# Graph network kernel, one core: four early output panels in place of three, ring of six entries, finished panels 26 units apart

## The chip, the cores and the metric

The kernel runs on one core of one Trainium2 chip. The metric is the device time of one execution in microseconds, lower is better. The time given for a kernel is the median of several executions; the profile is of one further execution.

## What is computed

Node features x are 8192 x 128, the adjacency matrix adj is dense 8192 x 8192, all in float32 (256 MB for adj). Two layers follow each other, each with a residual and a layer norm. Cut to what matters:

```python
# layer 0
A = a * adj; A[i, i] += 1 - a              # a = alpha[0]
deg = A.sum(axis=1)
x1 = layernorm(x + relu((A @ x) / deg @ W.T + b))
# layer 1
t = logmap0(x1)                            # row norms, log
par = adj   * sigmoid(left_par[:, None] + right_par[None, :])
chi = adj.T * sigmoid(left_chi[:, None] + right_chi[None, :])
u = chi @ t + par @ t
out = layernorm(x1 + proj(expmap0(u)))     # row norms, tanh
```

Layer 0 reads adj once. Layer 1 needs each block of adj twice, once as it lies and once transposed, and it needs t, which is made from layer 0's output.

## The kernel before, in words

The output is cut into 8 panels of 1024 nodes (NPAN = 8, BP = 1024) and the other axis of adj into 64 tiles of 128 rows (UPP = 64).

**Layer 0** goes panel by panel through 256 pairs (two tiles of adj, 1 MB, PPP = 32 pairs a panel). Of a pair, TensorE makes 8 matmuls into Y (line 1024) and VectorE adds its 128x2048 elements to the degree sums dsum (line 777). After a panel's 32 pairs its sum is taken to yb (line 782), and a chain of small steps, the passage, makes degrees, residual, norm, logarithm, tangent and scores of the panel. The passage of panel r - 1 runs among the pairs of panel r: constants T_... give the pair q (0 to 31) before which each engine makes its step. In it xT, the next panel's feature block, is loaded at T_LOADX and scaled at T_SCALEX (line 522), and the row of scores that a panel needs is written to HBM at tick 19 and read back to all partitions (two transfers of 512 KB) at tick 21 for each early panel.

**Layer 1** is cut into 512 units: a unit is one 128 x 1024 tile of the sum of both attention products for an output panel p. ScalarE makes two sigmoids (lines 613 and 627), GpSimd multiplies one by adj as it lies (line 477), VectorE multiplies the other by the transposed tile (line 868) and adds the two (line 879), and TensorE multiplies the sum with t into outp (4 matmuls, line 1092). Two units share two loads of 1 MB, "nat" and "trn".

**Early units.** A unit can start as soon as the t of its tile's panel is there. So EARLY = 3 output panels take units while layer 0 still runs: plan() places at most one unit at a pair, in groups of 8 to 24 units of one panel; at each group's end VectorE adds outp to acc (line 890, evacuate), and TensorE starts the next group only after that. With three early panels, 8, 12, 24, 32, 32, 24 and 24 units lie at the pairs of panels 1 to 7: 156 in all (N_EARLY). The other 356 run after layer 0, the first 12 of them as two more early groups, the rest as whole panels 3 to 7 with the last tiles of the early panels between them. The passage of panel 7 runs among the first 40 or so of these units, at twice the number of units.

**After layer 0.** Each finished output panel goes through a final chain (row norms, tanh, residual, layer norm, store), whose steps are given as F_... units after its base. FINALS holds the bases: 232, 266, 304, 338, 376, 410, 448 and 512.

**Loads.** SyncE issues all loads of adj in the order of use, each into the next entry of a ring of RING = 7 entries of 1 MB, and waits before each until the load that held this entry has been used: a pair by both line 1024 and line 777, a nat by both its units' products on GpSimd, a trn by those on VectorE. After layer 0, three more entries (EXTRA, where x lay) join.

Of the kernel before, what the change touches and what calls it, by code (L numbers as in the profile page):

```python
# [11 lines left out]
P = 128  # L12
D = 128
BP = 1024
NPAN = N // BP
TPP = BP // P
# [13 lines left out]
UPP = N // P  # L30
PPP = UPP // 2
PAIRS = NPAN * PPP
EARLY = 3
RING = 7
EXTRA = 3
CB = 3
KB = 3
# [6 lines left out]
(T_EVAC, T_FOLD, T_DEG, T_INV, T_LIN, T_RES, T_STATS, T_STD, T_RSTD, T_X1, T_SQ, T_NRM, T_LOGA, T_LN, T_FAC, T_XT,  # L44
 T_TURN, T_XTT, T_PRP, T_PRCR, T_ROWS, T_COPY, T_LOADL) = (0, 0, 1, 2, 3, 4, 5, 6, 7, 8, 9, 10, 11, 12, 13, 14,
                                                           16, 16, 17, 18, 18, 19, 21)
T_LOADX, T_SCALEX = 6, 10
T_UNITS = 20
T_OWN = 23

# [1 line left out]
def early_groups():  # L52

    groups = []
    for a in range(NPAN - 1):
        for p in range(min(EARLY, a + 1)):
            groups.append((p, range(0 if p == a else a * TPP, (a + 1) * TPP), a))
    return groups

def plan():

    unit_at, units, ends, waiting = {}, [], [], []
    groups = early_groups()
    for k, (p, tiles, a) in enumerate(groups):
        for jt in tiles:
            waiting.append((k, p, jt, (a + 1) * PPP + (T_OWN if p == a else T_UNITS)))
    for g in range(PAIRS):
        if waiting and waiting[0][3] <= g:
            k, p, jt, _ = waiting.pop(0)  # L70
            unit_at[g] = len(units)
            units.append((k, p, jt))
    n_early = len(units)
    units += [(k, p, jt) for k, p, jt, _ in waiting]
    order = []
    for k in range(EARLY, NPAN):
        order.append((k, range(UPP)))
        if k - EARLY < EARLY:
            order.append((k - EARLY, range((NPAN - 1) * TPP, UPP)))
    for p, tiles in order:  # L80
        groups.append((p, tiles, NPAN - 1))
        units += [(len(groups) - 1, p, jt) for jt in tiles]
    for n, (k, _, _) in enumerate(units):
        if n + 1 == len(units) or units[n + 1][0] != k:
            ends.append(n)
    return unit_at, units, n_early, groups, ends
# [17 lines left out]
def finals():  # L104
    out, base = [], {}
    for k, (p, tiles, a) in enumerate(GROUPS):
        if a == NPAN - 1:
            base[p] = ENDS[k] + 1
    for p in range(EARLY, NPAN):
        out.append((p, base[p]))  # L110
        if p - EARLY < EARLY:
            out.append((p - EARLY, base[p] + 34))
    return out

FINALS = finals()
FIN_OF = {p: k for k, (p, _) in enumerate(FINALS)}
F_EVAC, F_TURN, F_SLOT, F_COPY, F_SQUARE, F_ROOT, F_FLOOR, F_INV, F_RSTD, F_TANH, F_CHAIN, F_NORM, F_SCALE, F_ADD, \
    F_STATS, F_AGGR = 3, 2, 4, 5, 6, 15, 17, 18, 18, 19, 21, 20, 29, 31, 33, 42
F_LOADX = 16  # L120
F_STORE = 42
L_ROOT, L_RSTD, L_NORM = 47, 49, 52
F_STEPS = 8
# [63 lines left out]

def row_plan():
    out, use, end_of = {}, [0, 0, 0], [None, None, None]  # L190
    buf = 0
    for k, (p, tiles, a) in enumerate(GROUPS):
        if a < NPAN - 1:
            b = p
            if (p, "early") not in out:
                use[b] += 1
                out[(p, "early")] = (b, use[b], None)
        else:
            b = buf % 3
            buf += 1  # L200
            use[b] += 1
            out[k] = (b, use[b], end_of[b])
        end_of[b] = ENDS[k]
    return out
# [53 lines left out]
def adj_resnorm_kernel(nc, x_g, xT, g_blk, a_blk, WT, b_row, alpha, w_par, b_par, w_chi, b_chi, out):  # L258
    with ExitStack() as ctx:
        def sb(name, shape):  # L260
            return ctx.enter_context(nc.sbuf_tensor(name, shape, F32))

        def sem(name):
            return ctx.enter_context(nc.semaphore(name))
# [2 lines left out]
        xA = sb("xA", [P, N])  # L267
        xtA = sb("xtA", [P, N])
        acc = sb("acc", [P, EARLY * BP])
        scores = sb("scores", [P, 3, 2, BP])  # L270
        chi_few = sb("chi", [P, CB, BP])
        keys_few = sb("keys", [P, KB, BP])
        dsum = sb("dsum", [P, 2 * BP])
        yb = sb("yb", [P, BP])
        res = sb("res", [P, BP])
        xTt = sb("xTt", [P, BP])
        rows = xTt[0:2, :]

        prcr = sb("prcr", [P, UPP * 2])
# [58 lines left out]
        bpc2_ready = sem("bpc2_ready")  # L338
        x_in = [sem(f"x_in{G}") for G in range(NG)]
        r_in = [sem(f"r_in{e}") for e in range(RING + EXTRA)]  # L340
        l_in = [sem(f"l_in{k}") for k in range(3)]
        l0_used = sem("l0_used")
        deg_added = sem("deg_added")
        folded = sem("folded")
# [6 lines left out]
        h_ready = sem("h_ready")  # L351
# [14 lines left out]
        prp_ready = sem("prp_ready")  # L366
# [34 lines left out]
        def _(sp):  # L401
# [15 lines left out]
            def load_x1(k):  # L417
                p, _ = FINALS[k]
                if k < 2:
                    sp.wait_ge(x1_out, 16 * NPAN)  # L420
                    sp.wait_ge(xt_ready, NPAN)
                    sp.wait_ge(h_ready, NPAN)
                else:
                    sp.wait_ge(out_done, 16 * (k - 1))
                sp.dma_start(x1f[k % 2][:, :], x1_d[p]).then_inc(x1f_in[k % 2], 16)
# [86 lines left out]
        def _(act):  # L512

            def load_xT(r):
                if r > 0:
                    act.wait_ge(h_ready, r)
                act.dma_start(yb[:, :], xT[:, r * BP:(r + 1) * BP]).then_inc(xT_in, 16)

            def scale_xT(r):
# [16 lines left out]

            def squares(r):

                act.wait_ge(rows_out, 16 * r)
                for k in range(TPP):  # L540
                    ins = act.activation(xTt[:, k * D:(k + 1) * D], res[:, k * D:(k + 1) * D], ACT.Square,
                                         accum_out=ss[:, k:k + 1])
                ins.then_inc(ss_ready, 1)
# [614 lines left out]
```

## Time and profile before

| what | value |
|---|---|
| median of 3 runs | 2269.03 us (2265.76 to 2272.19) |
| profiled execution, device time | 2268.08 us |
| its span in the profile | 2266.1 us |
| PE busy | 1958.9 us, 86% of the span |
| VectorE (DVE) busy | 1992.6 us, 88% |
| ScalarE (ACT) busy | 1333.1 us, 59% |
| GpSimd (POOL) busy | 1307.4 us, 58% |
| moved by the DMA engines | 839.16 MB, 370 GB/s over the span |

The shares are averages over a first part (layer 0, up to 1269 us) and a second part whose limits differ, so that none of them names what binds; the stages have to be read one by one. The busy time of PE is modelled: matmuls overlap, and a busy PE is not PE at its peak.

### The profile page before, as it was taken

The page shows a single profiled execution, that of the slowest core. Times are in us where ns is not written, and L with a number is a line of the kernel's source. Part 1 is how long each engine was busy: PE and PEld are TensorE (multiplying, and loading weights), DVE is VectorE, ACT ScalarE, POOL GpSimd, SP SyncE. Part 2 cuts the span into 40 slices and gives each one's busy share as a digit, 9 for nine tenths or more (in the row PEclk, how much of TensorE's full clock was granted, in tenths as well). Part 3 has the DMA queues.
Part 4 walks back from the last instruction along what each step waited for, and adds up shares of the span by engine and source line. Part 5 has one row for each costly group of instructions (what it writes and reads, how often), then busy time and mean ns, then how long its engine had stood idle before and what let it go on. Part 6 is the DMA issues. An engine that isn't in the chain of part 4 may idle for free.

```text
span 2266.1 us, 17503 instructions
## 1 busy us (share of the span) xinstructions
PE 1958.9 (86%) x4652; PEld 827.4 (37%) x4652; DVE 1992.6 (88%) x1899; ACT 1333.1 (59%) x1622; POOL 1307.4 (58%) x544
## 2 busy tenths in 40 slices
PE   8999999999989989999999867887777777777774
PEld 3444444444434434444444322232232222222221
DVE  6676879989988988899899987999999999999995
ACT  0022134534543363354354587998889889898986
POOL 0001215325444444433433767989898998999995
PEclk9999999999999999999999999999999999999998
DMA  9988989999989898899999998999999999999994
GB/s 377 369 295 319 349 309 410 352 357 392 365 342 397 338 349 341 350 363 359 362 362 358 409 405 311 409 409 409 409 408 409 405 409 401 403 409 402 409 403 180
DMA packets 227568, 839.16 MB, mean 370 GB/s; under 512 B 14464, under 2 KB 22912, under 8 KB 227472
## 3 DMA queue, kind: packets, MB, share of 16 engines
q1 hardware_dynamic: 220672, 817.94, 92.7%
q10 hardware_dynamic: 6800, 20.13, 2.4%
q8 instruction: 38, 0.62, 0.1%
q14 instruction: 58, 0.48, 0.1%
HBM read 829.56 MB, written 8.45 MB: 370 GB/s over the span
## 4 chain that ended last, share of the span: by engine, by line
PE 34%; POOL 17%; issue 16%; DVE 15%; ACT 13%; DMA 4%; DVEq 0%; ACTq 0%; POOLq 0%; SPq 0%
PE ps L1024 25%; POOL chi L477 13%; PE ps L1092 7%; DVE dsum L777 6%; ACT chi L613 4%; DVE ps L868 4%; POOL xA L477 3%; ACT ps L627 3%; DMA ring<-in_a_cols 2%; DVE keys L879 1%; DMA ring<-in_g_blk 1%; ACT L613 1%; ACT xA L613 1%; DMA xA<-in_a_cols 1%; ACT dsum L657 1%
## 5 line engine op out<-in xcount | busy, mean ns | idle before, releaser
L477 POOL TENSOR_TENSOR chi<-chi,ring 128x1024 f32<-128x1024 f32 x322 | 812.3, 2536 | 741.0 <-ACT chi L613 620.9
L1092 PE MATMUL ps<-keys,xtA 128*128 128x512 f32 x1720 | 848.3, 620 | 198.7 <-DVE keys L879 169.4
L1024 PE MATMUL ps<-ring,xA 128*128 128x512 f32 x2048 | 921.7, 600 | 20.3 <-DMA ring<-in_g_blk 15.2
L627 ACT ACTIVATE ps<-scores,prcr 128x1024 f32<-128x1024 f32 x512 | 568.0, 1109 | 506.3 <-DVE keys L879 487.3
L777 DVE TENSOR_TENSOR dsum<-dsum,ring 128x2048 f32<-128x2048 f32 x240 | 595.8, 2482 | 23.8 <-DMA ring<-in_g_blk 18.4
L868 DVE TENSOR_TENSOR ps<-ps,ring 128x1024 f32<-128x1024 f32 x442 | 540.4, 1223 | 67.0 <-ACT ps L627 54.1
L879 DVE TENSOR_TENSOR keys<-ps,chi 128x1024 f32<-128x1024 f32 x430 | 526.5, 1224 | 59.2 <-issue 28.4
L1024 PEld LDWEIGHTS ps<-ring,xA 128*128 128x128 f32 x2048 | 390.2, 193 | 511.7 <-issue 489.7
L1092 PEld LDWEIGHTS ps<-keys,xtA 128*128 128x128 f32 x1720 | 315.3, 195 | 699.3 <-issue 659.8
L613 ACT ACTIVATE chi<-scores,prcr 128x1024 f32<-128x1024 f32 x430 | 488.2, 1135 | 7.5 <-DMA scores<-plcl_d 3.5
L477 POOL TENSOR_TENSOR chi<-chi,xA 128x1024 f32<-128x1024 f32 x108 | 254.5, 2374 | 36.5 <-ACT chi L613 33.6
L1092 PE MATMUL ps<-xA,xtA 128*128 128x512 f32 x328 | 159.7, 609 | 46.2 <-DVE xA L879 46.2
L477 POOL TENSOR_TENSOR xA<-xA,ring 128x1024 f32<-128x1024 f32 x50 | 118.8, 2375 | 11.5 <-ACT xA L613 9.0
L1092 PEld LDWEIGHTS ps<-xA,xtA 128*128 128x128 f32 x328 | 56.4, 190 | 146.7 <-issue 146.7
L879 DVE TENSOR_TENSOR xA<-ps,xA 128x1024 f32<-128x1024 f32 x82 | 100.4, 1225 | 3.7 <-POOL xA L477 1.0
L470 POOL TENSOR_TENSOR dsum<-dsum 128x1024 f32<-128x1024 f32 x8 | 18.8, 2351 | 136.9 <-DVE dsum L777 109.0
L613 ACT ACTIVATE xA<-scores,prcr 128x1024 f32<-128x1024 f32 x82 | 93.0, 1135 | 0.4 <-ACT xTt L567 0.4
L526 ACT ACT_TABLE_LOAD x8 | 10.3, 1283 | 140.2 <-PE ps L1040 140.1
L868 DVE TENSOR_TENSOR ps<-ps,xA 128x1024 f32<-128x1024 f32 x70 | 85.5, 1222 | 4.5 <-ACT ps L627 2.6
L477 POOL TENSOR_TENSOR xA<-xA 128x1024 f32<-128x1024 f32 x32 | 76.0, 2374 | 7.0 <-ACT xA L613 5.0
L773 DVE TENSOR_TENSOR dsum<-ring 128x1024 f32<-128x1024 f32 x16 | 25.2, 1618 | 29.4 <-PE ps L1033 18.3
L557 ACT ACTIVATE xtA<-res,small 128x128 f32<-128x128 f32 x64 | 19.6, 388 | 48.5 <-DVE small L839 48.5
(98 smaller groups left out, 618.2 us busy)
## 6 DMA issues: line engine op xcount, KB each, us to landing
ring<-in_g_blk SPq DMA_DIRECT2D x477, 1024.0 KB, 9.9
ring<-in_a_cols SPq DMA_DIRECT2D x186, 1024.0 KB, 12.3
xA<-in_a_cols SPq DMA_DIRECT2D x70, 1024.0 KB, 18.0
xA<-in_g_blk SPq DMA_DIRECT2D x35, 1024.0 KB, 18.2
scores<-plcl_d ACTq DMA_DIRECT2D x22, 512.0 KB, 6.8
xA<-in_x_g SPq DMA_DIRECT2D x16, 256.0 KB, 10.4
yb<-in_xT ACTq DMA_DIRECT2D x8, 512.0 KB, 6.7
x_d<-res ACTq DMA_DIRECT2D x8, 512.0 KB, 7.5
```

What stands on the lines that cost most here:

```text
L470: pool.tensor_tensor(out=dsum[:, 0:BP], in0=dsum[:, 0:BP], in1=dsum[:, BP:2 * BP], op=ALU.add).then_inc(folded, 1)
L477: pool.tensor_tensor(out=chi(n), in0=chi(n), in1=half(t, n), op=ALU.mult).then_inc(m2_ready, 1)
L557: ins = act.activation(xtA[:, at:at + D], res[:, k * D:(k + 1) * D], ACT.Copy, scale=fac[:, k:k + 1])
L613: act.activation(chi(n), scores[:, row, 1, :], ACT.Sigmoid, bias=prcr[:, 2 * jt + 1:2 * jt + 2]).then_inc(c_ready, 1)
L627: act.activation(slots[s], scores[:, row, 0, :], ACT.Sigmoid, bias=prcr[:, 2 * jt:2 * jt + 1]).then_inc(p_ready, 1)
L657: ins = act.activation(uT[:, i * D:(i + 1) * D], uN[:, i * D:(i + 1) * D], ACT.Square, accum_out=s_ss[:, k * TPP + i:k * TPP + i + 1])
L773: dve.tensor_tensor(out=half(dsum, h), in0=half(t0, h), in1=half(t, h), op=ALU.add) \
L777: dve.tensor_tensor(out=dsum[:, :], in0=dsum[:, :], in1=t, op=ALU.add).then_inc(deg_added, 1)
L868: dve.tensor_tensor(out=s, in0=s, in1=half(t, n), op=ALU.mult).then_inc(m1_ready, 1)
L879: dve.tensor_tensor(out=keys(n), in0=slots[SLOT_OF_UNIT[n][0]], in1=chi(n), op=ALU.add).then_inc(k_ready, 1)
L1024: ins = pe.matmul(Y[:, h * BANK:(h + 1) * BANK], xA[:, tile * D:(tile + 1) * D], t[:, tt * BP + h * BANK:tt * BP + (h + 1) * BANK], start= ...
L1092: ins = pe.matmul(outp[:, h * BANK:(h + 1) * BANK], xtA[:, jt * D:(jt + 1) * D], keys(n)[:, h * BANK:(h + 1) * BANK], start=begins, stop=i ...
```

## The change

A fourth output panel takes units among layer 0's pairs: 8, 12, 24, 32, 32, 32 and 32 units at the pairs of panels 1 to 7, 172 in all. 340 units run after layer 0, the first 52 of them in early groups (seven group ends against two before). LATE_BEHIND puts the early panels' last tiles behind panels 4 and 5, two behind each, and the bases of the final chains become 288, 314, 340, 368, 394, 420, 448 and 512.

The room for acc (4 KB more a partition) and for a fourth buffer of score rows (8 KB) comes from the ring, which goes from 7 to 6 entries (8 KB), and from xTt, which now shares yb's room (4 KB). Since xTt and yb are one, xT is loaded at tick 22 in place of 6 and scaled at 27 in place of 10, and some waits are added. The steps of the final chains move: the scaling on GpSimd from 29 to 27, the residual from 31 to 29, the statistics from 33 to 31, the load of x1 from 16 to 24.

```diff
--- before.py
+++ after.py
@@ -30,8 +30,8 @@
 UPP = N // P
 PPP = UPP // 2
 PAIRS = NPAN * PPP
-EARLY = 3
-RING = 7
+EARLY = 4
+RING = 6
 EXTRA = 3
 CB = 3
 KB = 3
@@ -44,7 +44,7 @@
 (T_EVAC, T_FOLD, T_DEG, T_INV, T_LIN, T_RES, T_STATS, T_STD, T_RSTD, T_X1, T_SQ, T_NRM, T_LOGA, T_LN, T_FAC, T_XT,
  T_TURN, T_XTT, T_PRP, T_PRCR, T_ROWS, T_COPY, T_LOADL) = (0, 0, 1, 2, 3, 4, 5, 6, 7, 8, 9, 10, 11, 12, 13, 14,
                                                            16, 16, 17, 18, 18, 19, 21)
-T_LOADX, T_SCALEX = 6, 10
+T_LOADX, T_SCALEX = 22, 27
 T_UNITS = 20
 T_OWN = 23
 
@@ -56,6 +56,11 @@
         for p in range(min(EARLY, a + 1)):
             groups.append((p, range(0 if p == a else a * TPP, (a + 1) * TPP), a))
     return groups
+
+
+
+LATE_BEHIND = {EARLY: (0, 1), EARLY + 1: (2, 3)}
+F_APART = 26
 
 
 def plan():
@@ -75,8 +80,8 @@
     order = []
     for k in range(EARLY, NPAN):
         order.append((k, range(UPP)))
-        if k - EARLY < EARLY:
-            order.append((k - EARLY, range((NPAN - 1) * TPP, UPP)))
+        for p in LATE_BEHIND.get(k, ()):
+            order.append((p, range((NPAN - 1) * TPP, UPP)))
     for p, tiles in order:
         groups.append((p, tiles, NPAN - 1))
         units += [(len(groups) - 1, p, jt) for jt in tiles]
@@ -108,16 +113,16 @@
             base[p] = ENDS[k] + 1
     for p in range(EARLY, NPAN):
         out.append((p, base[p]))
-        if p - EARLY < EARLY:
-            out.append((p - EARLY, base[p] + 34))
+        for i, early in enumerate(LATE_BEHIND.get(p, ())):
+            out.append((early, base[p] + (i + 1) * F_APART))
     return out
 
 
 FINALS = finals()
 FIN_OF = {p: k for k, (p, _) in enumerate(FINALS)}
 F_EVAC, F_TURN, F_SLOT, F_COPY, F_SQUARE, F_ROOT, F_FLOOR, F_INV, F_RSTD, F_TANH, F_CHAIN, F_NORM, F_SCALE, F_ADD, \
-    F_STATS, F_AGGR = 3, 2, 4, 5, 6, 15, 17, 18, 18, 19, 21, 20, 29, 31, 33, 42
-F_LOADX = 16
+    F_STATS, F_AGGR = 3, 2, 4, 5, 6, 15, 17, 18, 18, 19, 21, 20, 27, 29, 31, 39
+F_LOADX = 24
 F_STORE = 42
 L_ROOT, L_RSTD, L_NORM = 47, 49, 52
 F_STEPS = 8
@@ -187,7 +192,7 @@
 
 
 def row_plan():
-    out, use, end_of = {}, [0, 0, 0], [None, None, None]
+    out, use, end_of = {}, [0] * EARLY, [None] * EARLY
     buf = 0
     for k, (p, tiles, a) in enumerate(GROUPS):
         if a < NPAN - 1:
@@ -196,7 +201,7 @@
                 use[b] += 1
                 out[(p, "early")] = (b, use[b], None)
         else:
-            b = buf % 3
+            b = buf % EARLY
             buf += 1
             use[b] += 1
             out[k] = (b, use[b], end_of[b])
@@ -267,13 +272,14 @@
         xA = sb("xA", [P, N])
         xtA = sb("xtA", [P, N])
         acc = sb("acc", [P, EARLY * BP])
-        scores = sb("scores", [P, 3, 2, BP])
+        scores = sb("scores", [P, EARLY, 2, BP])
         chi_few = sb("chi", [P, CB, BP])
         keys_few = sb("keys", [P, KB, BP])
         dsum = sb("dsum", [P, 2 * BP])
         yb = sb("yb", [P, BP])
         res = sb("res", [P, BP])
-        xTt = sb("xTt", [P, BP])
+
+        xTt = yb
         rows = xTt[0:2, :]
 
         prcr = sb("prcr", [P, UPP * 2])
@@ -338,7 +344,7 @@
         bpc2_ready = sem("bpc2_ready")
         x_in = [sem(f"x_in{G}") for G in range(NG)]
         r_in = [sem(f"r_in{e}") for e in range(RING + EXTRA)]
-        l_in = [sem(f"l_in{k}") for k in range(3)]
+        l_in = [sem(f"l_in{k}") for k in range(EARLY)]
         l0_used = sem("l0_used")
         deg_added = sem("deg_added")
         folded = sem("folded")
@@ -420,6 +426,8 @@
                     sp.wait_ge(x1_out, 16 * NPAN)
                     sp.wait_ge(xt_ready, NPAN)
                     sp.wait_ge(h_ready, NPAN)
+                    sp.wait_ge(prp_ready, NPAN)
+                    sp.wait_ge(rows_out, 16 * NPAN)
                 else:
                     sp.wait_ge(out_done, 16 * (k - 1))
                 sp.dma_start(x1f[k % 2][:, :], x1_d[p]).then_inc(x1f_in[k % 2], 16)
@@ -514,6 +522,9 @@
             def load_xT(r):
                 if r > 0:
                     act.wait_ge(h_ready, r)
+                    act.wait_ge(prp_ready, r)
+                    act.wait_ge(rowp_ready, r)
+                    act.wait_ge(rows_out, 16 * r)
                 act.dma_start(yb[:, :], xT[:, r * BP:(r + 1) * BP]).then_inc(xT_in, 16)
 
             def scale_xT(r):
@@ -536,7 +547,7 @@
 
             def squares(r):
 
-                act.wait_ge(rows_out, 16 * r)
+                act.wait_ge(h_ready, r + 1)
                 for k in range(TPP):
                     ins = act.activation(xTt[:, k * D:(k + 1) * D], res[:, k * D:(k + 1) * D], ACT.Square,
                                          accum_out=ss[:, k:k + 1])
```

## Rows read from the trace of the kernel before

**Rows 1.** The page, part 1: busy time and share of each engine.
```profile
PE 1958.9 (86%) x4652; PEld 827.4 (37%) x4652; DVE 1992.6 (88%) x1899; ACT 1333.1 (59%) x1622; POOL 1307.4 (58%) x544
```

**Rows 2.** Windows, panels 3 to 7: length, busy (instructions) by engine, PEclk, DMA share, GB/s.
```profile
core 0: us, PE busy (x) PEld busy (x) DVE busy (x) ACT busy (x) POOL busy (x), PEclk, DMA share, GB/s
...
388.00:551.90 163.90, 161.46 (x413) 73.58 (x412) 147.57 (x131) 71.79 (x92) 67.89 (x26) 0.99 0.96 371
551.90:741.10 189.20, 178.50 (x445) 80.16 (x444) 167.89 (x147) 89.00 (x108) 87.71 (x34) 0.97 0.94 367
741.10:936.60 195.50, 183.26 (x447) 81.96 (x445) 171.19 (x150) 88.96 (x108) 87.75 (x34) 0.96 0.91 351
936.60:1102.90 166.30, 162.07 (x413) 74.52 (x412) 152.08 (x132) 71.78 (x92) 65.69 (x26) 0.99 0.92 357
1102.90:1269.20 166.30, 161.88 (x412) 74.06 (x413) 152.39 (x132) 71.79 (x92) 68.23 (x26) 0.99 0.93 359
```

**Rows 3.** Windows after layer 0: end of the last passage, and the steady part.
```profile
1350.00:1370.00 20.00, 15.36 (x28) 5.86 (x26) 19.34 (x23) 16.57 (x22) 14.83 (x7) 0.83 0.90 329
1370.00:1390.00 20.00, 12.81 (x35) 5.75 (x34) 13.44 (x12) 13.11 (x14) 13.25 (x7) 0.83 0.73 275
1390.00:1410.00 20.00, 16.17 (x44) 6.33 (x44) 15.42 (x15) 14.90 (x15) 14.96 (x7) 1.00 0.87 339
...
1430.00:1460.00 30.00, 24.68 (x52) 8.51 (x50) 29.55 (x26) 28.28 (x27) 30.00 (x14) 1.00 1.02 409
...
1493.00:2073.70 580.70, 439.63 (x926) 161.71 (x925) 546.64 (x577) 516.10 (x609) 529.92 (x228) 0.97 1.02 406
```

**Rows 4.** DMA issues from 1500 to 2200 us: count, size, median us to landing.
```profile
ring<-in_g_blk SPq DMA_DIRECT2D x104, 1024.0 KB, 18.5
```

**Rows 5.** DVE's timeline: the last panel's sum, and the last unit's key.
```profile
1269.21 1.27 DVE L782 SCALAR_TENSOR_TENSOR yb<-ps,alph,yb 128x1024 f32<-128x1024 f32 x1
...
2238.28 1.23 DVE L879 TENSOR_TENSOR keys<-ps,chi 128x1024 f32<-128x1024 f32 x1
```

**Rows 6.** Windows: pairs q = 14 to 21 of panels 5 and 6; pairs 20 to 30 of panel 7.
```profile
826.70:884.90 58.20, 50.58 (x125) 22.17 (x124) 46.38 (x38) 25.72 (x30) 26.79 (x11) 0.91 0.85 323
1019.10:1051.50 32.40, 32.03 (x93) 14.85 (x92) 29.09 (x25) 12.02 (x17) 7.69 (x3) 1.00 0.87 320
...
1211.00:1264.30 53.30, 53.30 (x125) 23.34 (x124) 51.35 (x31) 21.89 (x20) 28.84 (x11) 1.00 1.00 396
```

**Rows 7.** Waits of PE in panel 5's pairs 14 to 21: total, times, longest.
```profile
PE ps L1092 <- DVE acc L890: 4.5, 1, 4.5
PE ps L1060 <- DVE prcr L843: 3.1, 1, 3.1
```

**Rows 8.** Lines, panel 5 by form: busy, mean ns, then idle before.
```profile
L477 POOL TENSOR_TENSOR chi<-chi,ring 128x1024 f32<-128x1024 f32 x32 | 85.4, 2677 | 100.9 <-ACT chi L613 94.5 <-DMA ring<-in_a_cols 6.4
L777 DVE TENSOR_TENSOR dsum<-dsum,ring 128x2048 f32<-128x2048 f32 x30 | 76.0, 2533 | 0.0
```

**Rows 9.** One line's instructions, whole span: min/median/max ns.
```profile
L777 DVE TENSOR_TENSOR dsum<-dsum,ring x240: 2255/2292/4309, 18.0 to 1265.9; 128x2048 f32<-128x2048 f32 x120
...
L477 POOL TENSOR_TENSOR chi<-chi,xA x108: 2338/2366/2477, 1284.5 to 2219.2; 128x1024 f32<-128x1024 f32 x108
...
L890 DVE TENSOR_TENSOR acc<-ps,acc x15: 1211/1219/1225, 378.9 to 1312.9; 128x1024 f32<-128x1024 f32 x15
```

**Rows 10.** SyncE's timeline in panel 5: issues of the loads of pairs 11 and 12.
```profile
798.47 0.37 SPq L452 DMA_DIRECT2D ring<-in_g_blk  x1
806.90 0.37 SPq L452 DMA_DIRECT2D ring<-in_g_blk  x1
```

**Rows 11.** Issues at 798.47 and 806.90 us alone: us to landing.
```profile
ring<-in_g_blk SPq DMA_DIRECT2D x1, 1024.0 KB, 8.6
ring<-in_g_blk SPq DMA_DIRECT2D x1, 1024.0 KB, 4.8
```

**Rows 12.** Timeline of panel 5: PE at pair 11, GpSimd at pair 9's unit, xT's scaling.
```profile
803.20 3.67 POOL L477 TENSOR_TENSOR chi<-chi,ring 128x1024 f32<-128x1024 f32 x1 [2.05 <-ACT chi L613]
...
804.00 1.13 ACT L522 ACTIVATE yb<-yb,oma 128x1024 f32<-128x1024 f32 x1
...
807.42 3.60 PE L1024 MATMUL ps<-ring,xA 128*128 128x512 f32 x8
```

**Rows 13.** Waits of SyncE's queue in panel 5: total, times, longest.
```profile
SPq L452 <- DVE ps L868: 49.6, 14, 7.4
SPq L411 <- DVE dsum L777: 43.8, 14, 5.9
SPq L452 <- PE ps L1024: 32.4, 12, 8.5
SPq L452 <- POOL chi L477: 29.3, 8, 8.0
```

## The prediction

> **What bounds the kernel now.** I read the page first: VectorE 88% and TensorE 86% busy [rows 1], no engine full, so the stages have to be taken one by one. The timeline of VectorE cuts the run in two: layer 0 ends with the last panel's sum at 1269.2 us, the last unit's sum starts at 2238.3 us [rows 5], and the rest, up to 2266.1 us, is the last panel's final chain, which the change leaves alone.
>
> The windows after layer 0 show one limit. In the 580.7 us from 1493 on the DMA engines are saturated (share 1.02, 406 GB/s) while no engine is over 94% busy [rows 3]. A load waits 18.5 us from issue to landing [rows 4]. At the 409 GB/s of the window from 1430 to 1460 us [rows 3] a load of 1.0486 MB takes 2.563 us of the stream, so seven loads stand in the queue: the ring of ten is far deeper than this stage needs. A unit needs 1 MB there, and 2.563 us is its price. Only from 1350 to 1410 us, under the last passage, does the stream fall short (329, 275 and 339 GB/s [rows 3]): there the ring is full and the engines are what is late.
>
> Layer 0's windows are different. Panels 6 and 7 with 24 units take 166.3 us each, panels 4 and 5 with 32 units 189.2 and 195.5 us; the DMA share is 0.91 to 0.96, the TensorE clock 0.96 to 0.99 of full [rows 2]. In a stretch with no passage TensorE is busy all of 53.3 us with 125 matmuls, 0.426 us each [rows 6]: a pair with a unit (12 matmuls) costs 5.1 us, a pair alone 3.4. Two loads cost 5.13 us, so the two limits lie on top of each other there. In the passage's stretch neither holds: TensorE waits for engines.
>
> **The units that move: what they cost and what they save.** 16 units go from the late part to pairs, 8 to panel 6 and 8 to panel 7; panels 1 to 5 keep their counts.
>
> Saved after layer 0: 16 x 2.563 = 41.0 us, since that part is stream-bound behind the passage and the final chains move the same bytes as before.
>
> Added in layer 0: the 8 pairs that have no unit in panels 6 and 7 are q = 12 to 19, the densest part of the passage; with TensorE's two pairs of lag the products fall into q = 14 to 21. With units these 8 pairs took 58.2 us in panel 5, without 32.4 us in panel 6 [rows 6]: 25.8 us for 8 units, where 8 x 4 matmuls x 0.426 = 13.6 us would be TensorE's own work. The difference is waits: TensorE stands 4.5 us for a group's evacuation and 3.1 us behind the score step, once each [rows 7], and the clock is 0.91 there against 1.00. The whole panels carry the same message, and since the change makes panels 6 and 7 into copies of panels 4 and 5, I take those: the new panel 6 has group ends at q = 22 and 30, none at 14, like panel 4 (ends at 6 and 30), so 189.2 - 166.3 = 22.9 us; the new panel 7 has ends at 6, 14, 22 and 30 like panel 5, so 195.5 - 166.3 = 29.2 us. Together +52.1 us. Moved units thus cost 3.3 us each in place of 2.56. Bounds: 2 x 13.6 = 27.3 us if the units only cost TensorE's work, 2 x 29.2 = 58.4 us if both panels are like panel 5.
>
> Part of this price shows as two engines that slow each other: in panel 5 GpSimd's product takes 2677 ns and VectorE's dsum add 2533 ns on the mean [rows 8], against medians of 2366 and 2292 ns [rows 9]. The Trainium skill (SBUF, State Buffer, section Who interferes with whom) says that a VectorE instruction with two SBUF inputs and a GpSimd instruction that reads SBUF exclude each other for a whole instruction; the dsum add is such an instruction, while the two VectorE steps of a unit have one input in PSUM. By that rule the late part is free of it and each moved unit buys one possible collision, of at most a GpSimd product; the trace agrees in direction with the means just named. It speaks against the move, and its price is already inside the 52.1 us.
>
> **The ring of six in layer 0.** A load goes out when the entry that it takes is free. With one entry less and the same users, load i takes the entry that load i + 1 takes now, so it goes out when load i + 1 goes out in this trace. Where the next issue follows within 2.6 us nothing is lost, as the stream would not have been quicker. Panel 5 has one place where it matters: the load of pair 11 is issued at 798.47 us, the next, that of pair 12, only at 806.90 us [rows 10], when GpSimd has finished its product for the unit of pair 9 (803.20 + 3.67 = 806.87 [rows 12]) and so freed a nat entry. The first lands after 8.6 us, at 807.07; TensorE starts pair 11 at 807.42 [rows 11, 12], with 0.35 us to spare. With six entries it goes out at 806.90 and with the 4.8 us that a load issued then takes [rows 11] lands at 811.7 us: TensorE and the dsum add behind it stand 4.3 us. Nothing gives this back, since TensorE has 5.1 us of work a pair afterwards and the later loads wait for users that are late too. SyncE waits for VectorE, TensorE and GpSimd in turn [rows 13], so every entry is held to the end of its use. The passage repeats in every panel, the normalisation and squares on ScalarE that make GpSimd late at that place too, so I count 4.3 us in each of panels 3 to 7: +21.5 us. Bounds: nothing, if the six entries suffice after all (panels 1 and 2, with few units, I count so); and 5 x (4.3 + 2.1) = 32 us, should each panel have a second place half as costly, some 40 with a clock that falls after the waits.
>
> After layer 0 the ring is 9 entries instead of 10. It is full when the passage ends, so the stream starts its last, saturated run one load behind: +2.6 us. Further on, with seven loads in flight now, six suffice: nothing. If that cover were gone, each final chain would cost a load, 8 x 2.6 = 20 us.
>
> **Group ends.** An evacuation is 1.219 us on VectorE [rows 9]. During the late passage there are now five more ends of early groups. VectorE is 19.3 of 20 us busy in one of the three windows and 13.4 and 15.4 in the next [rows 3], so some of the five fall into its idle time: I take 3 us. Bounds: 0, and 5 x (1.2 + 0.4) = 8.
>
> **Transfers.** The fourth early panel's score rows are one more MB, at tick 21 of panel 4, where stream and TensorE are even: up to 2.6 us. The load of xT (0.5 MB, 1.3 us) moves from tick 6, where the stream has room, to tick 22, where it has none, in four panels of 32 units: up to 5 us, less what the earlier stretch gains. I take +2, bounds 0 and 8. ScalarE's scaling at tick 27 (1.13 us [rows 12]) and the waits added to load_xT, load_x1 and squares are on work that is done ticks before: ScalarE is 89.0 of 195.5 us busy in panel 5 [rows 2]. Nothing; without that cover, one wait of some 3 us a panel.
>
> **Final chains 26 apart.** GpSimd needs 26 x 2.366 us [rows 9] plus two operations of that size for its chain, 66 us; the stream needs 26 x 2.563 + 2.56 us for x1 and the store, 69.2 us. The stream still sets the pace. VectorE: 546.6 us busy for 216 units and six chains [rows 3], 2.53 us a unit with chains in; 26 x 2.53 = 66 us, and a little more with chains denser: also below. Nothing; bound 10 us if steps of two chains meet in the queues.
>
> **The sum.** Against the profiled execution of 2268.08 us: + 52.1 - 41.0 + 21.5 + 2.6 + 3 + 2 = + 40.2, 2308.3 us. The median of the runs is 1 us higher, so 2309 us.
>
> **The rivals.**
> 1. *The ring of six costs nothing* and only the rest holds: 52.1 - 41.0 + 2.6 + 3 + 2 = +18.7, 2288 us. For it: the stalls rest on one place that I read with 4.3 us, and xT's scaling leaves ScalarE just ahead of it, which brings GpSimd's product forward by up to 1.1 us. Against: the product that frees the entry waits for sigmoids that the ring doesn't touch. Chance 0.2.
> 2. *Faster: the moved units cost TensorE's work alone*, 27.3 us, against 41.0 saved, because the waits of panels 4 and 5 in the passage belong to where their groups end and not to the units. With the other terms and a harmless ring, 27.3 - 41.0 + 2.6 + 2 = -9, about 2260 us. It decides below (41.0 - 8)/16 = 2.1 us a unit. Against: panel 4 has no group end at q = 14 and still is 22.9 us over panel 6. Chance 0.12; a mixture that lands within 0.3% 0.08.
> 3. *The late part loses its saturation*: chains that overlap at 26 units, nine entries. Another 10 to 20 us on the forecast, 2325 us. Against: seven loads in the queue. Chance 0.1.
>
> My forecast, both the panels' price and the ring's, has 0.5.
>
> **How the numbers follow.** The forecast's own range, from the bounds of its terms, is 2292 to 2328 us. For 8 in 10 it has to take in the first rival and reach toward the second: 2268 to 2330. Within 0.3% (6.8 us, about what a measurement of this kernel can tell from no change) I give 0.08, faster 0.12, slower 0.5 + 0.2 + 0.1 = 0.8.
>
> **What would show it.** In the profile after: panels 6 and 7 of 190 to 200 us (175 to 180 would be rival 2); panels 3, 4 and 5 4 us longer than 163.9, 189.2 and 195.5 with TensorE waiting for ring<-in_g_blk near q = 11 (unchanged: rival 1); layer 0's last sum at about 1345 us; from there to the end 962 us in place of 997, with the stream at 405 to 409 GB/s once the passage is over (less: rival 3). The prediction is wrong if the passage's waits don't grow with the units, or if ScalarE without xT's scaling at tick 10 frees the entries in time.

## The result and the profile after

The changed kernel takes 2298.07 us (median of 4 runs, 2293.92 to 2302.52) against 2270.61 us for the kernel before beside it: ratio 1.0116, 95% interval 1.0097 to 1.0135. It is slower, by 26 us by the ratio (27 by the two medians), on the side that was forecast and inside the range; the forecast was 40 us. The profiled execution's span is 2292.1 us against 2266.1, so the profiles differ by 26.0 us too and can be read against each other term by term.

The page of the changed kernel, part 1 (answers to [rows 1]):

```profile
PE 1963.1 (86%) x4656; PEld 825.3 (36%) x4656; DVE 1990.1 (87%) x1903; ACT 1334.7 (58%) x1622; POOL 1318.1 (58%) x544
```

No engine got much more work: the busy times differ by some 4 us at most on PE, VectorE and ScalarE, and by 11 on GpSimd, which is idle for 42% of the span. The 26 us are for the most part waits. Windows of panels 3 to 7 of the changed kernel, as in [rows 2]:

```profile
391.43:562.85 171.42, 162.51 (x414) 73.31 (x412) 148.77 (x132) 71.85 (x92) 68.45 (x26) 0.99 0.92 357
562.85:754.68 191.83, 178.58 (x445) 80.02 (x444) 168.41 (x147) 89.16 (x108) 89.47 (x34) 0.97 0.93 361
754.68:944.69 190.01, 177.65 (x443) 79.71 (x442) 171.26 (x149) 89.14 (x108) 89.77 (x34) 0.97 0.93 359
944.69:1132.48 187.79, 177.91 (x446) 80.06 (x445) 166.83 (x148) 89.15 (x108) 87.81 (x34) 0.97 0.94 365
1132.48:1323.83 191.35, 179.22 (x445) 80.07 (x444) 171.65 (x150) 89.03 (x108) 91.72 (x34) 0.97 0.92 358
```

Panel by panel against [rows 2]: +7.5, +2.6, -5.5, +21.5, +25.1 us, and 3 to 4 us in panels 0 to 2. VectorE's timeline gives the two cuts, the last panel's sum and the last unit's key (answers to [rows 5]):

```profile
1323.83 1.27 DVE L793 SCALAR_TENSOR_TENSOR yb<-ps,alph,yb 128x1024 f32<-128x1024 f32 x1
...
2264.32 1.23 DVE L890 TENSOR_TENSOR keys<-ps,chi 128x1024 f32<-128x1024 f32 x1
```

Layer 0 ends 54.6 us later (1323.8 - 1269.2), and from there to the last key it is 940.5 us in place of 969.1, 28.6 us less; the tail is the same 27.8 us. 54.6 - 28.6 = 26.0.

The late part, in windows of the changed kernel (the last passage, the time just after it, the steady part) as in [rows 3]:

```profile
1430.00:1460.00 30.00, 22.56 (x61) 9.73 (x60) 21.14 (x19) 16.31 (x16) 14.73 (x7) 0.89 0.74 281
1488.00:1518.00 30.00, 23.58 (x50) 8.23 (x49) 29.59 (x26) 27.57 (x27) 30.00 (x14) 1.00 1.03 409
1518.00:2100.00 582.00, 439.75 (x929) 159.54 (x929) 540.50 (x571) 517.41 (x610) 525.39 (x226) 0.98 1.02 407
```

The stream is as saturated as before once the passage is over (407 GB/s, share 1.02): nine entries and chains 26 units apart did not take that away. Under the passage it falls to 281 GB/s, as it fell to 275 in the kernel before [rows 3].

### The profile page after: what moved, and what is told of

It reads as the page before. It is cut to its first block, busy times and chain, and to the rows that moved or that the text cites. A ratio compares the mean times of both kernels' runs of the same rounds, so it can differ in the third digit from the quotient of the medians.

```text
span 2292.1 us, 17535 instructions
## 1 busy us (share of the span) xinstructions
PE 1963.1 (86%) x4656; PEld 825.3 (36%) x4656; DVE 1990.1 (87%) x1903; ACT 1334.7 (58%) x1622; POOL 1318.1 (58%) x544
## 4 chain that ended last, share of the span: by engine, by line
PE 27%; issue 18%; POOL 18%; DVE 17%; ACT 15%; DMA 5%; DVEq 0%; ACTq 0%; POOLq 0%; SPq 0%
PE ps L1035 20%; POOL chi L485 14%; DVE ps L879 6%; DVE dsum L788 6%; ACT chi L624 5%; PE ps L1103 5%; POOL xA L485 3%; ACT ps L638 3%; DMA ring<-in_a_cols 2%; DMA xA<-in_a_cols 2%; DVE keys L890 1%; DMA ring<-in_g_blk 1%; ACT L624 1%; ACT xA L624 1%; PE ps L1071 1%
## 5 line engine op out<-in xcount | busy, mean ns | idle before, releaser
L485 POOL TENSOR_TENSOR chi<-chi,ring 128x1024 f32<-128x1024 f32 x349 | 886.5, 2553 | 758.2 <-ACT chi L624 474.0
L1103 PE MATMUL ps<-keys,xtA 128*128 128x512 f32 x1736 | 852.9, 616 | 196.2 <-DVE keys L890 161.8
L879 DVE TENSOR_TENSOR ps<-ps,ring 128x1024 f32<-128x1024 f32 x398 | 486.7, 1223 | 81.0 <-ACT ps L638 43.2
L485 POOL TENSOR_TENSOR chi<-chi,xA 128x1024 f32<-128x1024 f32 x85 | 200.0, 2365 | 30.5 <-ACT chi L624 26.9
L1103 PE MATMUL ps<-xA,xtA 128*128 128x512 f32 x312 | 153.5, 615 | 44.6 <-DVE xA L890 44.6
L879 DVE TENSOR_TENSOR ps<-ps,xA 128x1024 f32<-128x1024 f32 x114 | 139.3, 1222 | 8.6 <-ACT ps L638 6.2
L890 DVE TENSOR_TENSOR xA<-ps,xA 128x1024 f32<-128x1024 f32 x78 | 95.5, 1225 | 3.3 <-POOL xA L485 0.8
L485 POOL TENSOR_TENSOR xA<-xA 128x1024 f32<-128x1024 f32 x27 | 63.9, 2368 | 3.4 <-DMA xA<-in_a_cols 2.8
L784 DVE TENSOR_TENSOR dsum<-ring 128x1024 f32<-128x1024 f32 x16 | 18.9, 1222 | 29.3 <-PE ps L1044 18.3
## 6 DMA issues: line engine op xcount, KB each, us to landing
xA<-in_a_cols SPq DMA_DIRECT2D x56, 1024.0 KB, 16.1
```

The lines of the kernel that those rows point to most:

```text
L485: pool.tensor_tensor(out=chi(n), in0=chi(n), in1=half(t, n), op=ALU.mult).then_inc(m2_ready, 1)
L784: dve.tensor_tensor(out=half(dsum, h), in0=half(t0, h), in1=half(t, h), op=ALU.add) \
L879: dve.tensor_tensor(out=s, in0=s, in1=half(t, n), op=ALU.mult).then_inc(m1_ready, 1)
L890: dve.tensor_tensor(out=keys(n), in0=slots[SLOT_OF_UNIT[n][0]], in1=chi(n), op=ALU.add).then_inc(k_ready, 1)
L1103: ins = pe.matmul(outp[:, h * BANK:(h + 1) * BANK], xtA[:, jt * D:(jt + 1) * D], keys(n)[:, h * BANK:(h + 1) * BANK], start=begins, stop=i ...
```

## The experiments

Each was timed beside the kernel before, whose median was 2271.2, 2272.7 and 2268.3 us in three groups of runs. Ratios carry their 95% interval. Times of single panels come from one profile of each kernel, and two profiles of the same kernel can differ: layer 0 ends at 1323.8 us in the first profile of the changed kernel and at 1332.6 in the second (after_again). A difference of a few us in one panel is read as one only where several profiles show it.

| run | what it is | ratio | interval |
|---|---|---|---|
| e1_ring6 | 3 early panels, 6 entries | 1.0079 | 1.0061 to 1.0096 |
| e2_late_xt | 3 early, 7 entries, late xT | 0.9984 | 0.9973 to 0.9996 |
| e3_ring6_late_xt | 3 early, 6 entries, late xT | 1.0087 | 1.0072 to 1.0102 |
| e4_four_ring7 | 4 early, 7 entries | 1.0073 | 1.0056 to 1.0090 |
| after_again | the changed kernel | 1.0109 | 1.0090 to 1.0128 |
| e5_withheld | changed, 16 units held back | 1.0116 | 1.0096 to 1.0136 |
| e6_merged | changed, 3 group ends fewer | 1.0081 | 1.0062 to 1.0099 |
| e7_three_withheld | before, 16 units held back | 0.9936 | 0.9920 to 0.9952 |
| e8_withheld_merged | the same, ends merged | 0.9948 | 0.9932 to 0.9965 |
| e9_hold_12_16 | before, pairs 12 to 16 free | 1.0084 | 1.0068 to 1.0100 |
| e10_hold_15_19 | before, pairs 15 to 19 free | 1.0101 | 1.0085 to 1.0118 |
| e11_held_merged_late_xt | e8 with late xT | 0.9941 | 0.9927 to 0.9956 |

**The parts of the change, one by one.** e1 changes one line of the kernel before, `RING = 7` to `RING = 6`.

> The kernel before with six ring entries and nothing else. My theory (each of panels 3 to 7 gets one TensorE stall of 4.3 us near pair 11, nothing gives it back, and the late stream starts one load behind): layer 0's end 21 us later, the whole +24 us, ratio 1.0105. Rival (panels 4 and 5 already stand for loads at pairs 12 and 13, 4 us each, and the new stall takes the place of that one): panels 4 and 5 unchanged, panels 3, 6 and 7 +4 to +7 us each, the whole +15 us, ratio 1.0065. Rival (six entries suffice): +3 us, ratio 1.001.

+18 us, between the theory's 24 and the rival's 15. Windows of its panels 3 to 7:

```profile
391.27:561.56 170.29, 162.46 (x414) 73.24 (x412) 148.73 (x131) 71.78 (x92) 68.84 (x26) 0.99 0.94 360
561.56:751.68 190.12, 179.38 (x445) 80.41 (x444) 170.97 (x147) 88.99 (x108) 89.69 (x34) 0.97 0.93 362
751.68:944.74 193.06, 179.70 (x442) 80.89 (x443) 172.34 (x150) 88.97 (x108) 89.92 (x34) 0.96 0.91 351
944.74:1115.63 170.89, 164.09 (x414) 74.28 (x413) 152.46 (x132) 71.78 (x92) 68.69 (x26) 0.98 0.90 347
1115.63:1288.23 172.60, 162.57 (x411) 73.64 (x410) 151.39 (x132) 71.77 (x92) 70.98 (x27) 0.98 0.92 356
```

The 24-unit panels 3, 6 and 7 pay 6.4, 4.6 and 6.3 us, the 32-unit panels 4 and 5 +0.9 and -2.4. The first three panels together take 3.3 us more, where nothing was counted. So the loss exists and has about its forecast size, but in a panel filled with units it is given back: the rival of the shifted stall, by its panels if not quite by its total. From layer 0's end on, the run is 3.5 us longer (2.6 were forecast).

e2 and e3 load xT late, with seven and with six entries:

```diff
-T_LOADX, T_SCALEX = 6, 10
+T_LOADX, T_SCALEX = 22, 27
...
-        xTt = sb("xTt", [P, BP])
+        xTt = yb
```

and the waits of the change's diff on load_xT, load_x1 and squares.

> The kernel before with xT loaded at tick 22 and scaled at tick 27, xTt in yb's room, seven entries. My theory (a hidden transfer is moved from one covered place to another): within 3 us of before. Rival (xT's 0.5 MB at tick 6 and its scaling at tick 10 are part of what makes the loads of pairs 12 and 13 late in panels 4 and 5): these two panels 4 us shorter each, the whole -8 us, ratio 0.9965.

> Both: six entries and the late xT, three early panels. If the two act apart, the sum of the two runs before it. My theory: +24 us, ratio 1.0105. Rival of a shifted stall: +7 to +15 us, ratio 1.003 to 1.0065, with TensorE waiting near pair 10 and no longer at 12 and 13.

The late xT is 3.6 us faster by the ratio with seven entries, and makes no measurable difference with six (1.0079 and 1.0087). The rival's place is right: pairs 12 and 13 together take 11.3 us in e2's panel 4 and 10.9 in its panel 5, in place of 14.5 and 14.2. But other waits of the same panels grow, TensorE's for a group's evacuation in panel 5 from 4.5 to 6.1 us, and the panels take 188.6 and 194.7 us, not 4 us less than 189.2 and 195.5. What makes the 3.6 us stays open.

e3 against e2 is also the ring's price with late xT and three early panels: 1.0087 - 0.9984, 23 us. By panels (3 to 7: +6.6, 0.0, -3.7, +7.4, +6.5 us, and +2.3 before them) it repeats what e1 shows.

e4 is the changed kernel with RING = 7. The room comes from score rows: three buffers, the early units of panel 3 reading panel 0's rows. The kernel leaves out the early read-back of panel 3's own rows, 1 MB in panel 4. In that panel the step from pair 22 to pair 23 takes 6.6 us in the changed kernel and 5.1 to 5.2 in the kernel before and in e4, so some 1.4 us of the difference between e4 and the changed kernel may be this transfer and not the ring.

```diff
-RING = 6
+RING = 7
...
-            b = p
+            b = p % 3
...
-                if tick == T_LOADL and r < EARLY:
+                if tick == T_LOADL and r < 3:
```

> The changed kernel with seven ring entries; the room comes from score rows, of which three buffers stay: the early units of panel 3 read panel 0's score rows, and panel 3's own are not read back early. My theory (ring 24 us, moved units and group ends the rest): 2274 us, +4 us against before, panels 6 and 7 still over 185 us. Rival (the ring costs less than 10 us, the moved units make most of the loss): +15 us or more, ratio 1.007 or more. A ratio below 1 would say that the moved units gain and the ring alone makes the change slower.

> The changed kernel once more, on the chip of the runs beside it, so that they can be compared with it. Ratio 1.0116 within its interval. Against the run with four early panels and seven entries (1.0073) it gives what the seventh entry is worth in the changed kernel: 10 us by the ratios, 4 us by the two profiles.

With seven entries four early panels still cost 17 us against before and 20 against e2, where the theory had 4: the ring alone doesn't explain the loss. The seventh entry is worth 8 us here (1.0109 - 1.0073; the intervals just touch) where it is worth 18 with three early panels (e1), 23 with late xT (e3 against e2): the two losses overlap. The profiles agree: e4's panels 3 to 7 take 165.2, 188.8, 191.1, 190.6 and 196.3 us. Six entries cost panel 3 6.3 us and panel 4 3.0, and make panels 5, 6 and 7 1.1, 2.8 and 5.0 us shorter; with after_again in place of the first profile it is 9.8 and 2.8 dearer, then 1.2, 2.3 and 2.5 shorter. Layer 0 ends 3 and 12 us behind e4's.

**The moved units.** e5 (in the changed kernel, panels 6 and 7) and e7 (in the kernel before, panels 4 to 7, of which 4 and 5 had such units) leave pairs 12 to 19 without units:

```diff
-        if waiting and waiting[0][3] <= g:
+        if waiting and waiting[0][3] <= g and not (g // PPP >= 4 and 12 <= g % PPP < 20):
```

(`>= 6` in e5; the 16 units then run behind layer 0).

> The changed kernel without units at pairs 12 to 19 of panels 6 and 7: the 16 moved units go back behind layer 0, everything else stays, six entries and four early panels among it. By my prediction's price (3.3 us a unit in layer 0, 2.56 behind it, 3 us for two more group ends) it is 8 us faster than the changed kernel, ratio about 1.008. Theory after the first runs (with six entries panels 6 and 7 would be 171 to 173 us without the units and are 188 and 191 with them, so 2.2 us a unit): 6 us slower than the changed kernel, and the group ends on top, ratio about 1.015.

> The kernel before without units at pairs 12 to 19 of panels 4 and 5: 16 units go from layer 0 to behind it, seven entries, three early panels. The stretch is what made the forecast's price: 22.9 and 29.2 us for 8 units each. If that is the price of units there, panels 4 and 5 fall to 166 us each, layer 0 ends 50 us earlier, the rest is 41 us longer and two more group ends cost 3 us: ratio 0.997. Rival (the waits belong to those panels or to the group ends, and the units cost TensorE's work of 13.6 us a panel): ratio 1.006.

e5 gives nothing, against both expectations: 1.0116 against 1.0109. Panels 6 and 7 fall to 172.3 and 168.5 us from 188.3 and 193.8 in the changed kernel's run beside it, 41.3 us for 16 units, 2.6 each, and the late part grows by 47, with two group ends more. (Against the first profile it is 38.3 us, 2.4 each.) At six entries a unit costs about the same on either side.

e7 is 14.5 us faster than the kernel before, the clearest gain of the study and twice what was expected. Its panels 3 to 7:

```profile
388.24:552.99 164.75, 160.60 (x414) 73.25 (x413) 150.51 (x132) 71.78 (x92) 67.96 (x26) 1.00 0.96 370
552.99:714.74 161.75, 158.89 (x411) 72.69 (x410) 147.35 (x131) 71.77 (x92) 69.20 (x26) 1.00 0.96 370
714.74:881.18 166.44, 163.40 (x416) 74.61 (x414) 151.52 (x131) 71.78 (x92) 64.62 (x26) 0.99 0.94 364
881.18:1047.15 165.97, 159.92 (x413) 73.06 (x412) 151.41 (x133) 71.78 (x92) 65.36 (x26) 1.00 0.93 360
1047.15:1213.32 166.17, 160.89 (x411) 73.39 (x411) 150.76 (x132) 71.78 (x92) 68.91 (x26) 0.99 0.93 358
```

Panels 4 and 5 go from 189.2 and 195.5 us to 161.8 and 166.4: 56.5 us for 16 units, 3.5 each. The price that the prediction read off whole panels (3.3) is the units', not the panels': the same two panels lose it when the units go. TensorE's own work would have been 27 of the 56 us. The clock rises from 0.97 and 0.96 to 1.00 and 0.99 with it. The rest of the run grows by 46 us, for these units and the two group ends that move behind layer 0 with them. GpSimd's product and VectorE's dsum add take 2639 and 2530 ns on the mean in e7's panel 5, against 2677 and 2533 in the kernel before's: the slowing of each by the other, which the prediction named, is as large per instruction without the 8 units as with them, so it does not explain why units are dearer here than behind layer 0 by more than each product's own 0.3 us.

**The group ends.** e6 merges the last early groups of the changed kernel, so that four ends in place of seven lie behind layer 0:

```diff
+    last = NPAN - 2
+    groups = [g for g in groups if g[2] < last and (g[2] < last - 1 or g[0] == 0)]
+    for p in (1, 0, 2, 3):
+        groups.append((p, range((last - (p > 0)) * TPP, (last + 1) * TPP), last))
```

> The changed kernel with the last early groups merged (panels 1, 2 and 3 take tiles 40 to 55 in one group each), so that four group ends in place of seven lie behind layer 0; units, pairs and loads as they are. If the ends cost what the late passage grew by (9 us for five more), the part up to unit 60 behind layer 0 shrinks by 4 to 6 us, ratio 1.009 to 1.010. If an end is hidden (1.2 us of an engine that idles there), less than 1 us. If the stream and not the passage sets the time, the part shrinks and the whole doesn't.

1.0081 against 1.0109, 6 us, though the two intervals overlap a little (up to 1.0099, and from 1.0090). By the times of VectorE's last step of a unit (the sum into keys), the first 60 units behind layer 0 take 185.4 us in the kernel before, 194.5 in the changed one, 192.5 in its second run and 185.9 in e6. So five ends more cost 7 to 9 us and three fewer give back 7 to 9: more than 1.2 us of VectorE each. PE's waits show the other half, over the first 60 units of the kernel before (1269 to 1465 us), then from layer 0's end to 1520 us in the changed kernel and in e6:

```profile
PE ps L1092 <- DVE acc L890: 5.7, 2, 4.2
```

```profile
PE ps L1103 <- DVE acc L901: 13.7, 6, 4.2
```

```profile
PE ps L1107 <- DVE acc L905: 6.5, 3, 3.7
```

Two such waits have become six, 8.0 us more: TensorE stands at each end some 2 us until VectorE has added its accumulator to acc, and the last passage has TensorE steps between its units. e8 does the same to e7 (with p in 1, 0, 2 and three ends left behind layer 0):

> The kernel with pairs 12 to 19 free of units (ratio 0.9936), and its last early groups merged, so that three group ends in place of four lie behind layer 0 and two in place of three in panel 7. Merging three ends gave 6 us in the changed kernel, 2 us each: 2 to 4 us faster, ratio 0.992. Rival (an end is hidden here): 0.9936.

0.9948 against 0.9936: no gain. Its first 60 late units are 2.8 us shorter, but layer 0 ends 7 us later in its profile, all of it in panels 0 to 4, where the two kernels are the same. And e11 below, with the same ends as e8, takes as long for its first 60 units as e7 (190.4 and 190.3 us). A merged end is not worth anything that this could measure on top of e7.

**Where in the stretch the price lies.** e9 keeps only pairs 12 to 16 free, e10 only 15 to 19; each puts 27 units in each of panels 4 to 7 in place of e7's 24.

> The kernel before with only pairs 12 to 16 of panels 4 to 7 free of units: three units a panel run at pairs 17 to 19. Theory A (a unit is dear where its sigmoids stand ahead of the passage's steps at ticks 14 to 18): the three are past the dear steps and cost TensorE's 1.7 us, 3 to 8 us gained on 12 units against the kernel with 12 to 19 free, ratio 0.990 to 0.993. Rival (units are dear anywhere in the stretch, 3.3 us): 9 us slower than that kernel, ratio 0.9975.

> The kernel before with only pairs 15 to 19 of panels 4 to 7 free of units: three units a panel run at pairs 12 to 14, whose products come at pairs 14 to 16. Theory A: the score step at tick 17 has no sigmoids ahead of it any more, ratio 0.992 to 0.995. Rival (the dear places are the loads of pairs 12 and 13 and the group's end at 14, 10 us of the 26): ratio 0.997 to 1.0.

Both are far slower than either theory allows, 34 and 37 us slower than e7 for 12 units that return. The windows of panels 4 to 7 say why, first e9, then e10:

```profile
552.30:725.85 173.55, 167.43 (x424) 75.66 (x423) 155.27 (x136) 78.32 (x98) 77.18 (x30) 0.98 0.96 369
725.85:917.13 191.28, 174.52 (x425) 79.12 (x424) 156.73 (x137) 78.32 (x98) 76.24 (x28) 0.94 0.83 324
917.13:1089.63 172.50, 166.52 (x428) 75.66 (x426) 157.72 (x138) 78.42 (x98) 72.68 (x29) 1.00 0.97 373
1089.63:1278.80 189.17, 170.27 (x421) 76.58 (x422) 158.29 (x138) 78.31 (x98) 77.86 (x29) 0.95 0.84 327
```

```profile
549.37:736.17 186.80, 173.66 (x427) 77.39 (x425) 155.58 (x136) 78.16 (x98) 78.81 (x29) 0.96 0.87 338
736.17:910.07 173.90, 165.83 (x422) 75.40 (x422) 156.16 (x138) 78.17 (x98) 74.67 (x29) 0.99 0.94 363
910.07:1099.82 189.75, 173.56 (x428) 77.30 (x426) 160.19 (x139) 78.28 (x98) 77.66 (x29) 0.96 0.85 331
1099.82:1275.62 175.80, 164.33 (x421) 74.65 (x422) 157.15 (x138) 78.17 (x98) 74.51 (x29) 1.00 0.93 359
```

Every second panel is 13 to 19 us dearer, panels 5 and 7 in e9, 4 and 6 in e10, with the DMA share at 0.83 to 0.87. Two units share a nat and a trn. Panel 4 begins with unit 44 and panel 5 with unit 71; e9's gap comes after 12 units, at 56 and 83, e10's after 15, at 59 and 86. Where that number is odd, the gap parts two units that share their loads, and two of the seven entries stay held over five pairs for a unit still to come. The alternation swaps between the two runs as this asks, and SyncE's queue shows the held entry: its waits for GpSimd's product, total, times and longest, in panels 4 and 5 of e9, then of e10:

```profile
SPq L452 <- POOL chi L477: 16.1, 6, 8.1
SPq L452 <- POOL chi L477: 58.6, 13, 25.2
```

```profile
SPq L452 <- POOL chi L477: 46.1, 12, 19.6
SPq L452 <- POOL chi L477: 47.5, 10, 8.6
```

The longest is 20 to 25 us in the four dear panels and 7 to 9 in the other four. In these, three units cost 6.5 to 11.8 us over the same panel of e7, 2.2 to 3.9 each, in either half of the stretch. So these two runs don't settle which pairs are dear; they show what two missing entries do.

e11 adds the late xT to e8:

> The merged and withheld kernel with the late load of xT and xTt in yb's room. The late load gave 0.9984 alone, mostly in panels with units at pairs 12 to 14, which have none here: no difference within 2 us. If it keeps its 3.5 us, this is the fastest, ratio 0.990.

0.9941: the three kernels with the stretch free of units are equal within their intervals, some 13 us faster than the kernel before and 39 us faster than the changed one.

## Why the prediction was right, and by how much its terms were off

**The size, by parts.** By the ratios, with the late xT in all of them but e1, six entries alone cost 23 us (e3 against e2; 18 without the late xT, e1), the fourth early panel alone 20 (e4 against e2), and both together 28 to 30, where 43 would be their sum. The forecast had 24.1 for the ring (21.5 + 2.6) and 16.1 for the rest, which e4 measures as 17 against the kernel before. Each part alone came out near its forecast; what was wrong was to add them. On top of four early panels the ring costs 8 us, and that accounts for the 14 us between 40 and 26. The sum is also helped by two errors of opposite sign: layer 0 grew by 54.6 us where 75.6 was forecast (its last sum at 1324 us and not 1345), and the rest shrank by 28.6 where it was 35.4 (968 us and not 962). The range of 2292 to 2328 us is a judgement: the bounds given for the terms add up to about 2255 to 2372.

**Two regimes.** Right. The late part is bound by the stream: behind the last passage (from unit 60 after layer 0) the changed kernel is 37.7 us shorter, forecast 41.0 - 2.6 = 38.4, at 407 GB/s. The denser chains cost nothing that shows. One load behind at the start was right too: behind unit 60 e1 takes 2.4 us more than the kernel before, and e3 2.8 more than e2.

**The moved units.** The forecast set panels 6 and 7 at 189.2 and 195.5 us plus the ring's 8.6, +60.7 us together; they came out at 187.8 and 191.3, +46.6. With seven entries they are 190.6 and 196.3 (e4), so it is the ring's part that is missing. The units' price of 3.3 us holds with seven entries (3.5 by e7; by e4's panels against e2's 54.6 us for the 16, 3.4 each), but with six it is 2.2 to 2.6 (the changed kernel against e1, and e5). Against 2.56 behind layer 0 it is a loss in the first case and a draw in the second.

**The ring: the step that failed is "nothing gives this back".** In panel 5 the place, the cause and the size of the wait were as forecast. TensorE's timeline of the changed kernel there, at pairs 10 and 11:

```profile
813.76 3.60 PE L1035 MATMUL ps<-ring,xA 128*128 128x512 f32 x8
...
823.37 6.56 PE L1035 MATMUL ps<-ring,xA 128*128 128x512 f32 x8 [4.30 <-DMA ring<-in_g_blk]
```

A wait of 4.30 us where 4.3 was worked out, for the load that goes out after GpSimd's product of 3.67 us. But in a 32-unit panel other waits shrink behind it. The steps from one pair's start to the next, by the first matmuls of the pairs, in panel 5:

| pair | 10 | 11 | 12 | 13 | 14 | 17 |
|---|---|---|---|---|---|---|
| before | 5.2 | 5.1 | 7.2 | 7.0 | 11.6 | 12.0 |
| e4, seven entries, four early panels | 5.2 | 5.1 | 7.4 | 7.0 | 11.3 | 10.4 |
| changed | 9.6 | 8.1 | 5.1 | 5.1 | 6.3 | 12.8 |

Two waits of the kernel before lie behind that place, one for the load of pair 13 and one for a group's evacuation:

```profile
819.76 5.40 PE L1024 MATMUL ps<-ring,xA 128*128 128x512 f32 x8 [1.88 <-DMA ring<-in_g_blk]
...
834.84 3.63 PE L1092 MATMUL ps<-keys,xtA 128*128 128x512 f32 x4 [4.53 <-DVE acc L890]
```

PE's waits in pairs 14 to 21 as [rows 7], in the changed kernel (841.7 to 900 us):

```profile
PE ps L1071 <- DVE prcr L854: 4.1, 1, 4.1
PE ps L1103 <- DVE acc L901: 0.9, 1, 0.9
```

The wait for the load of pair 13 is gone, and the one for the evacuation has gone from 4.5 to 0.9 us: TensorE now comes later to what was late anyway. In e1 the evacuation's wait stays (3.6 us), and pairs 12, 13 and 17 shrink, to 5.3, 5.3 and 9.1 us. In a 24-unit panel there are no such waits behind pair 11, and the price stays: +7.5 in panel 3, 6.4, 4.6 and 6.3 in e1.

Not all of the 5.5 us by which panel 5 of the changed kernel is shorter is the ring's. With four early panels its 32 units fall into other groups, with three group ends in place of four, and e4, with seven entries, already takes 191.1 us there, 4.4 less than the kernel before. The prediction kept panel 5 as it was; the smaller ring itself takes off 1.1 (against e4) to 3.7 us (e3 against e2).

The change turns two of the three 24-unit panels into 32-unit ones, so the stall had to be counted in full once (panel 3) and not five times. The term was +21.5; against e4, layer 0 ends 3 and 12 us later in the two profiles.

**Group ends.** Right in kind, too small: +3 us was taken; the first 60 late units grew by 9.1 us in the first profile and 7.1 in the second, and e6 ties this to the ends. The prediction counted VectorE's time alone and left out TensorE's wait at each end (8.0 us more in all). The bound, 8, was from the same count.

**Transfers.** +2 was taken. The late xT alone is not a cost (0.9984). The fourth panel's score rows have no run of their own; the step from pair 22 of panel 4 puts them at some 1.4 us.

**The rivals.** The first, six entries are free, is refuted by e1. The second, TensorE's work alone (1.7 us a unit), is refuted by e7, and with six entries by e5. The third, a late part out of saturation, didn't occur. The sum of the measured terms is +8 in panels 0 to 5, +46.6 in panels 6 and 7, +9.1 under the last passage and -37.7 behind it, 26 us.

## What to carry to other kernels

Work that fills idle slots has a price that can be read: compare the same stage with and without it, whole, and set that against what it costs where it runs now. Here 16 units cost 56 us in slots that looked free and 46 us elsewhere, and taking them out gave more than any other edit tried here. Stalls on one path need not add: before a stall is multiplied by the number of stages, look in each kind of stage for a later wait that it can slip under. And when work that shares a buffer is paused, pause it at a boundary of the buffer, or it holds the buffer through the pause.

## What was not expected of the hardware

```profile
823.40:829.90 6.50, 6.50 (x9) 2.82 (x10) 5.56 (x9) 2.60 (x3) 2.98 (x2) 0.56 1.03 420
813.80:819.00 5.20, 5.20 (x13) 2.05 (x11) 4.04 (x4) 5.14 (x6) 3.67 (x1) 1.00 0.79 323
```

The granted clock is 0.56 behind the wait, most of the window at the lower level (1.2 GHz), and 1.00 before it. That makes this stall dearer than its wait, by up to 3 us. The kernel before, too, has longer matmuls behind its waits: 5.40 us for 8 matmuls after 1.88 us, and 3.63 in place of 1.88 us for a unit's four after 4.53. The clock of whole panels goes with the waits: 0.96 and 0.97 in the 32-unit panels of the kernel before, 1.00 and 0.99 in the same two in e7. The prediction had named such a fall in a bound only.
